# One gather of expert results per attention head in place of two, a later second one in two heads, and the weighted sums placed ahead of the first products of the last head

## What is computed

```python
xn = _layernorm(x, axis=-1)
x = x + _L0_attn_ref(xn, ...) + _L0_ffn_ref(xn, ...)

# attention
scores = jnp.einsum('bhqd,bhkd->bhqk', q, k) * scale
scores = jnp.where(cam[None, None, None, :], scores, neg)
attn = jax.nn.softmax(scores, axis=-1)
out = jnp.einsum('bhqk,bhkd->bhqd', attn, v)
out = out.transpose(0, 2, 1, 3).reshape(b, s, HID)
return jnp.einsum('bsd,ed->bse', out, Wo) + bo

# experts
expert = top_idx[:, 0]
weight = top_w[:, 0]
act = jax.nn.silu(gate) * up
out_e = jnp.einsum('eti,ehi->eth', act, down_w)
combine = jax.nn.one_hot(expert, e, dtype=x.dtype) * weight[:, None]
out = jnp.einsum('eth,te->th', out_e, combine)
```

## Time and profile before

| what | us |
|---|---|
| median of 3 runs | 394.4 |
| lowest and highest of them | 393.45, 394.83 |
| the profiled execution | 396.47 |
| its span, first to last instruction | 394.7 |
| PE busy (94% of the span) | 370.9 |
| DVE busy (82%) | 322.2 |
| ScalarE (ACT) busy (68%) | 270.2 |
| POOL busy (17%) | 65.6 |

### The profile page before, as it was taken

One profiled execution on the slowest core, in us unless ns is written; L12 is line 12 of the kernel. 1 busy time (PEld: TensorE's weight loads), 2 busy tenths in 40 slices (PEclk: granted clock), 3 DMA queues, 4 the chain that ended last, 5 costly groups with the idle time before them and its releaser, 6 DMA issues.

```text
span 394.7 us, 12245 instructions
## 1 busy us (share of the span) xinstructions
PE 370.9 (94%) x4646; PEld 194.1 (49%) x4646; DVE 322.2 (82%) x549; ACT 270.2 (68%) x537; POOL 65.6 (17%) x82
## 2 busy tenths in 40 slices
PE   0999999999999999999999999999999999997896
PEld 0765566766655443444444444445454444432265
DVE  5769789997759888988888888888888898874566
ACT  2534666564448878778787787878888888886910
POOL 5003734431000213032130321300000000000000
PEclk9999999999999999999999999999999999998999
DMA  7998556755111213032130321302102022095626
GB/s 238 407 384 215 145 169 200 215 171 157 41 58 54 70 32 95 11 94 63 41 88 14 99 55 46 92 11 71 55 21 70 25 52 56 17 204 105 101 54 213
DMA packets 30920, 42.53 MB, mean 108 GB/s; under 512 B 10724, under 2 KB 25700, under 8 KB 30048
## 3 DMA queue, kind: packets, MB, share of 16 engines
q1 hardware_dynamic: 29000, 36.71, 32.5%
q0 software_dynamic: 1872, 5.11, 5.1%
HBM read 27.75 MB, written 13.67 MB: 105 GB/s over the span
## 4 chain that ended last, share of the span: by engine, by line
PE 83%; DMA 5%; DVE 4%; issue 3%; ACT 2%; SPq 2%; DVEq 0%; ACTq 0%
PE ps L735 19%; PE ps L713 18%; PE ps L653 17%; PE ps L601 7%; PE ps L528 5%; PE ps L614 5%; PE ps L772 4%; DVE mx L1025 3%; DMA softmax_sums<-o_st 2%; DMA bqk<-bqk_in 2%; PE ps L639 2%; PE ps L517 1%; PE ps L587 1%; PE ps L626 1%; PE ps L510 1%
## 5 line engine op out<-in xcount | busy, mean ns | idle before, releaser
L1025 DVE TENSOR_REDUCE mx<-ps 128x1 f32<-128x717 f32 x232 | 198.6, 899 | 30.6 <-PE ps L653 30.1
L735 PE MATMUL ps<-q_op,k_op 98*32 98x512 bf16 (+1 forms) x1472 | 129.7, 383 | 3.6 <-DMA q_op<-neg_row 1.6
L1307 ACT ACTIVATE probs<-ps 128x512 f32<-128x512 f32 x192 | 103.1, 598 | 19.9 <-PE ps L735 18.1
L653 PE MATMUL ps<-k_op,q_op 96*32 96x512 bf16 (+1 forms) x1856 | 111.2, 315 | 0.4 <-DVE mx L1025 0.3
L653 PEld LDWEIGHTS ps<-k_op,q_op 96*32 96x32 bf16 x1856 | 50.7, 96 | 56.3 <-issue 25.3
L735 PEld LDWEIGHTS ps<-q_op,k_op 98*32 98x32 bf16 (+1 forms) x1472 | 42.3, 96 | 67.0 <-ACT probs L1307 15.0
L713 PE MATMUL ps<-probs,v_op 128*32 128x512 f32 x384 | 50.6, 595 | 0.2 <-ACT o_st L1298 0.2
L1307 ACT ACTIVATE dn<-ps 77x512 f32<-77x512 f32 x64 | 34.8, 595 | 11.6 <-PE ps L735 11.6
L457 POOL COPY v_op<-v_all 128x192 f32<-128x192 f32 x16 | 7.0, 446 | 202.7 <-PE ps L713 202.7
L1307 ACT ACTIVATE gu<-ps 128x512 f32<-128x512 f32 x64 | 34.5, 599 | 9.1 <-PE ps L735 9.1
L1307 ACT ACTIVATE wqk<-ps 128x512 f32<-128x512 f32 x64 | 33.5, 599 | 8.1 <-PE ps L735 8.1
(11 more groups left out here) (127 smaller groups left out, 366.0 us busy)
## 6 DMA issues: line engine op xcount, KB each, us to landing
q_parts<-parts SPq DMA_DIRECT2D x12, 256.0 KB
sorted_results<-ys SPq DMA_DIRECT2D x23, 128.0 KB
q_op<-q_parts SPq DMA_DIRECT2D x15, 192.0 KB
gu<-gu_in SPq DMA_DIRECT2D x1, 2816.0 KB, 13.7
tab<-tab_in SPq DMA_DIRECT2D x1, 2048.0 KB, 11.6
sorted_rows<-xn SPq DMA_DIRECT2D x4, 512.0 KB, 6.1
out<-x_sb SPq DMA_DIRECT2D x8, 256.0 KB, 2.4
q_op<-q_parts SPq DMA_DIRECT2D x15, 128.0 KB
```

Of the source, the lines that this page charges most:

```text
L653: ins = pe.matmul(ps[r:r + CW, at + c0:at + c0 + n], q_op[slot][0:KR, P * t + r:P * t + r + CW], k_op[slot][0:KR, c0:c0 + n], start=True, ...
L735: ins = pe.matmul(bank(4 + u % RING)[r:r + w, :], k_op[k][:, c0 + r:c0 + r + w], q_op[k][:, QB * b:QB * b + QB], start=True, stop=True)
L1025: dve.tensor_reduce(mx[:, slot, t:t + 1], ps[:, at:at + NK], AX.X, ALU.max).then_inc(max_reduced, 1)
L1307: act.activation(prob[c][0:rows, QB * b:QB * b + QB], bank(4 + u % RING)[0:rows, :], ACT.Exp, scale=SCALE).then_inc(exp_done, 1)
```

## The change

POOL's loop now runs over heads 0 to 13 (it acts while PE is in the head after): a copy of v where there is still one to make, one gather, one bias addition. After heads 7 and 8 a second tile follows (tiles 14 and 15): there POOL waits for two more chunks `P` of the running head before it makes the first addition, then gathers the second tile and makes the second addition. There are 16 gathers and 16 additions as before. On DVE the 16 weighted sums stand ahead of the four `divide` of heads 0 to 7. PE, ACT and SP have the same instructions in the same order.

```diff
+TWO_GATHERS = (7, 8)
...
+            def add_bias(t):
                 pool.tensor_tensor(x_sb[:, t, :], x_sb[:, t, :], bvo[:, HID:2 * HID], ALU.add
                                    ).then_inc(residual_ready, 1)
 
-            for h in range(RING, HEADS):
-                pool.wait_ge(pv_done, (h - 2) * NCH)
-                copy_v(h, h % RING)
-                for t in range(2 * (h - RING), min(2 * (h - RING) + 2, NT)):
-                    gather_result(t)
+            for h in range(HEADS - 2):
+                pool.wait_ge(pv_done, (h + 1) * NCH)
+                if h + RING < HEADS:
+                    copy_v(h + RING, h % RING)
+                gather_result(h)
+                if h in TWO_GATHERS:
+                    pool.wait_ge(pv_done, (h + 1) * NCH + 2)
+                    add_bias(h)
+                    gather_result(HEADS - 2 + TWO_GATHERS.index(h))
+                    add_bias(HEADS - 2 + TWO_GATHERS.index(h))
+                else:
+                    add_bias(h)
...
-            dve.wait_ge(attn_in[0], 16 * (1 + HEADS // 2))
-            for b in range(NQB):
-                divide(0, 0, P, b, attn_ready)
-
             dve.wait_ge(residual_ready, NT)
             dve.wait_ge(gathered, 16 * NT)
             for t in range(NT):
                 dve.scalar_tensor_tensor(x_sb[:, t, :], y_tok[:, t, :], tk["weight"][:, t:t + 1],
                                          x_sb[:, t, :], ALU.mult, ALU.add).then_inc(y_added, 1)
+            dve.wait_ge(attn_in[0], 16 * (1 + HEADS // 2))
+            for b in range(NQB):
+                divide(0, 0, P, b, attn_ready)
+
```

## The result

On the chip of the first comparison the changed kernel took 391.92 us (median of 20 runs, 390.15 to 393.88) against 395.52 for the kernel before in the same rounds (20 runs, 392.85 to 398.15): ratio 0.9914, interval 0.9891 to 0.9936, 3.6 us less. The profiled execution took 391.15, its span is 389.3. In three later sets, on chips 0, 6 and 4, the ratio was 1.0059, 0.9939 and 0.9934; the first of these is on the other side, and the experiments are largely about that. The chip of the first comparison has no number here; it may be one of these three.

What follows compares the result with a forecast made beforehand. Bound by each head's path: PE's tile 14, two DVE reductions, two negations, turn. Terms -4.90 + 0 + 1.0 + 0.5 + 0 = -3.4 took 394.4 to 391.0 us, range 389.5 to 393.2.

Steps and rivals of the forecast that it cites:

- The path of a head and the 4.90 us: Heads 1 to 8: tile 14, two reductions, two negations, turn; POOL's two tiles cost 0.61 a head, 4.90 in all.
- What holds it back: the additions.: Within a head: a DVE instruction due at an addition's start or during it begins 0.4 to 0.75 after that start.
- the hold: Late start of DVE's reductions, put on POOL's additions: 0.33 at the third, 0.49 to 0.83 at the fourth.
- cost per gather: Rival: each of 16 gathers costs 0.31 wherever its addition stands, and head 14 adds 0.5; 394.9 us, chance 0.07.
- Twelve heads with one gather, 0.: Heads 1 to 7 and 10 to 14: the addition touches only the third reduction, which has slack; 0, at most 1.8.
- nothing in a plain head waits for a DMA: Reason given why gathers outside head 14 would cost nothing: they only change heads, whose instructions need no transfer; no cost.
- Heads 8 and 9, +0.5 each: First addition runs 4.97 to 5.72, beside DVE's negations, and delays the turn; 1.0 for both, 0 to 2.0.
- the forecast's paragraph on the rule: Skill's rule clears additions of late reductions; a two-input negation would wait until 5.72, costing heads 8 and 9 0.9.
- Head 14, +0.5: Path into head 15: the last gather meets full DMA engines and delays the sums; 0.5, between 0 and 1.0.
- The clock at head 15: 0.5 more PE idle changes neither the clock's fall nor, probably, its 3.6 us; half as long again would add 0.85.
- the cases: Forecast 390.2 to 392.3, 0.60; larger gain 389.5, 0.15; smaller 393.1, 0.13; by gather 394.9, 0.07; slower 398.5, 0.05.
- The order of the sums, 0: DVE's weighted sums ahead of the products: both still fit before PE wants the products, with 8 us of cover; cost 0.

Runs made afterwards that it cites:

- gathers alone: Kernel before with all 16 additions made ahead of the heads and a memset in each one's place; 391.9 us on chip 0, 398.71 on chip 6.
- Additions alone: Kernel before with a memset in place of each gather in heads 1 to 8, gathers moved to heads 9 to 12; 394.58 us on chip 0.
- the pair on chip 6: Changed kernel unchanged, 391.16 us, ratio 0.9939; and the same with DVE's weighted sums put back behind the four divides, 390.87, ratio 0.9931.

## Why the prediction was right, point by point

The forecast was 391.0 from 394.4, 3.4 less. Measured were 3.6 less, 391.9 from 395.5. The sum was nearly right, and the reason given for its largest term was wrong. That the sum came so close is in part luck: the heads gave 0.5 less than forecast, the 0.5 set for head 14 was not seen, and the kernel ran where the gather costs something; on chip 0 the same reasoning would have missed by 5.5.

- **The path of a head and the 4.90 us.** Right. The loss is at the fourth reduction and at the turn, and eight heads give it back: -3.39 measured over the twelve heads between the copies, where 4.90 less 1.0 was expected, -3.9. The 0.5 that is missing lies in an early head (16.14), in head 11 (16.25) and in a few hundredths elsewhere.
- **"What holds it back: the additions."** This step failed. An addition begins within 0.03 of the end of its gather, so most rows fit both. One did not: the fourth reduction was due at 3.30, before the second addition begins at 3.38 and while the second gather was on, yet the forecast counted it as due "at an addition's start". The gathers alone gave the whole hold on chip 6, and with the gathers alone, without a memset, reductions were late on chip 4. Additions alone were never run on a chip with the hold, so that they add nothing to it there is argued from the equal sizes, not shown. The rival "cost per gather" named the true instruction, though not the way (its rows land too late for it), and had the price wrong: its 0.31 for each gather was a mean over the first, whose lateness has slack, and the second, which is paid. The forecast's own reasoning, that a place on the path counts, gave the time.
- **Twelve heads with one gather, 0.** Right for the mechanism it spoke of: the third reduction starts late by up to 0.36 (at 2.24) and the fourth is on time at 3.30, except once, on chip 4, where it began at 3.43 behind a third at 2.22 and that head was 16.09 long. What it missed is the sentence that nothing in a plain head waits for a DMA. A maxima tile in the middle of head 11 does, in the changed kernel:

```profile
301.19 0.49 PE L663 MATMUL ps<-k_op,q_op 96*32 96x512 bf16 x8 [0.17 <-DMA k_op<-k_parts]
```

  Head 11 was 15.96, 16.17, 16.17 and 16.02 long in the four traces without a gather in it, and 16.18 to 16.71 in those with one. That a gather in head 11 makes the load later fits these figures, and was not tested by itself.
- **Heads 8 and 9, +0.5 each.** Right in place and size: 16.46 in every trace of the changed kernel (once 16.49), 0.50 over the plain head, and 15.96 once the additions were gone on chip 0. The shape was another. POOL, DVE and PE of the changed kernel, head 8: the addition begins at 252.03 and ends at 252.76 (rows above), and

```profile
252.12 0.67 DVE L1041 TENSOR_SCALAR neg<-mx 128x16 bf16<-128x16 f32 x1
252.83 0.17 DVE L1044 SCALAR_TENSOR_TENSOR neg<-mx,neg 128x16 bf16<-128x16 f32 x1
```

```profile
253.15 0.22 PE L670 MATMUL ps<-id,neg 128*32 128x128 bf16 x1 [0.48 <-issue]
```

  The first negation did not start late. It started on time and lasted 0.67 instead of 0.17, to 0.03 behind the end of the addition. The second follows at once and takes its usual 0.17, so the one that waited was not the one with two inputs, which the forecast's paragraph on the rule and the expectations of later runs had named. The first negation is held by the addition, and the reductions by the gather: two different waits, which the forecast had taken for one.
  The Trainium skill, "SBUF — State Buffer", section "Who interferes with whom", says that a VectorE instruction with two SBUF inputs, or one in a two-port mode, can be shut out by a GpSimd instruction that reads SBUF until that is done, and that `tensor_reduce` does not contend. The 0.67 fits the clause on two-port modes, since the instruction has one SBUF input; that it ran in such a mode no run here shows. The clause on two inputs is not tested, as the addition was over when the second negation began. The second half, which the prediction had set aside because of rows 3 to 5, agrees with the additions alone on chip 0: in the head from 187.58 the fourth reduction starts at 3.30 in the middle of an addition that lasts from 2.80 to 3.53.
- **Head 14, +0.5.** Not seen. The last gather went out at 344.38, 16.2 behind the last copy of v and so where the forecast had it (347.5 in a kernel 3.3 longer up to there), and the sums were stored in 8.3 us instead of 9.2 (timeline of SP after, beside the earlier trace rows):

```profile
346.27 0.59 SPq L366 DMA_DIRECT2D softmax_sums<-o_st  x1
...
354.53 0.36 SPq L373 DMA_DIRECT2D sum_c<-softmax_sums  x1
354.94 0.66 SPq L361 DMA_DIRECT2D q_op<-neg_row  x1
```

  From the first scores of head 14 to the first scores of head 15, five traces without a gather in that head gave 14.7 to 16.6 and nine with one 14.7 to 16.2. The scatter of 2 us is far above 0.5; whether there is such a term stays open.
- **The clock at head 15.** The forecast took it for unchanged. It fell behind idle times of PE of 1.58 (before) and 1.74 (gathers alone, chip 6) and not behind 1.29, 1.16, 1.13, 1.10 and 0.78. In the first pair of traces this is 1.2 of the 2.04 beyond the sum, and the shorter idle time 0.8. It comes and goes with the transfers of the executions, and no run here tells whether the change itself makes it rarer.
- **The order of the sums, 0.** Right as far as the pair on chip 6 can tell.

That the change is slower on chip 0 was in none of the cases. The forecast's terms explain it with one put to zero: without the hold, 4.90 becomes 0 and the +1.0 of heads 8 and 9 stays.

## What to carry to other kernels

Where two instructions always stand together in a trace, a late start beside them is no evidence for either; look for the one head in which they are apart, or make one, before giving the cost a cause. What counted was the place: the same hold cost nothing at the third reduction, 0.5 at the fourth, and 0.77 where the seventh and an exponential were due, because of who waited behind it. And when an engine starts late, look at what it waits for before calling the engine itself slow: here two engines were late together, and the signal of a third was the cause. Before a gain of 1% is trusted, let it run on more than one chip: here it was 0.6 to 0.9% in three sets and a loss of 0.6% on chip 0.

## What the runs showed of the hardware

- In the first comparison and on chips 6 and 4, a gather of 128 rows of 256 float32 on GpSimd made PE's semaphores late that were to be raised about its end: they came 0.26 to 0.83 us behind that end, and DVE's reductions and ScalarE's exponentials that wait for them started late with them. Semaphores raised by DVE and ScalarE were not late. On chip 0 nothing of it was seen. What the engines share there, and why one chip is free of it, stays open: the gather's first packet goes out from about 0.7 us behind the instruction's end on either kind, so their own pace does not tell the chips apart.
- A negation of 16 columns took 0.67 to 0.71 us in place of 0.17 beside an addition on GpSimd, in heads 8 and 9 of all five traces with that order, chip 0 included, and neither negation was late behind a gather that ended 0.13 before the first was due.
- No version run here is the best everywhere: the changed kernel loses to the kernel before on chip 0, by 2.1 us. Its twin with the sums behind was level with it on chip 6, the only chip on which it was run.
